# Pair slots of a vision tower's last block: norm weights behind the transposes, rows scattered from the residual, value projection behind the value products

## The chip, the core and the metric

The kernel runs on one core of one Trainium2 chip. A core has TensorE (PE: matmuls and transposes, with PEld its weight loads), VectorE (DVE), ScalarE (ACT), GpSimd (POOL) and SyncE (SP, which here only starts transfers). The engines run their own instruction streams in order and meet at semaphores. The metric is the device time of one execution in microseconds (us), the median of several runs; lower is better.

## The reference, cut to what matters

64 images become 49 tokens of 192 numbers each (a patch embedding), pass a window attention, and then the block that the change touches:

```python
h = tok(x, ...)                                   # patch embedding: (64, 49, 192)
h = h + attn(_layernorm(h), ...)                  # windows attention
h = h + ffn(_layernorm(h), ...)                   # the block below

def ffn(x, ...):                                  # x is the normalised h
    xn = _layernorm(x, norm1_w, norm1_b)
    q, k, v = split(xn @ qkv_w.T + qkv_b)         # 12 heads of 16
    o = softmax(q @ k.T * scale) @ v
    x = x + (o @ proj_w.T + proj_b)
    xn2 = _layernorm(x, norm2_w, norm2_b)         # second norm
    top_vals, top_idx = top_k(xn2 @ w_gate, 2)    # 2 of 8 experts per token
    gates = softmax(top_vals)
    for e in range(8):                            # computed only for the chosen ones in the kernel
        moe += gate[e] * (gelu(xn2 @ W1[e] + b1[e]) @ W2[e] + b2[e])
    return x + moe
```

## The kernel before

The program has four stages. The patch embedding and the window attention come first and are not touched. Then come the **pair slots** (class `Heads`, its methods `gpsimd`, `vector`, `scalar` and `tensor`): 32 pairs of images, a pair being one tile of 128 rows (2 x 64, 49 of each 64 real). After them the **expert tiles**: the token rows, sorted by expert in a DRAM buffer `xs_d`, go through in 56 tiles of 128 rows. Last, every pair fetches its two expert rows per token and adds them to the residual.

The pair slots are a software pipeline written out by hand: `run_slots` calls a function `slot(item)` once per step on every engine, and `item(lag)` is the pair that entered `lag` steps ago. So one slot holds work of up to eight pairs. Slots 0 to 7 and 32 to 38 are unrolled, 8 to 31 are a hardware loop of two slots a turn. Within a slot each engine's order is the order of the lines, and nothing else reorders it:

- lag 0: VectorE takes mean and variance of the residual row block (L619 bn_stats, L633 bn_aggr). GpSimd turns the variance into two inverse roots in six tiny instructions with a drain between each (L507 to L517, "the root chain"), since the block's input is itself a normalised row. VectorE forms the normalised rows (L648), ScalarE scales them again (L804), TensorE transposes them (L943), ScalarE applies the first norm's weight and bias while it copies them out of PSUM, per partition, since the features are on the partitions there (L807).
- lag 1: query and key projections (L898), value projection (L907), ScalarE copies queries (L794) and values (L814) out, VectorE spreads the keys (L644).
- lag 2: scores (L880), maximum and subtraction on VectorE (L624, L629), exponential (L786), transposes (L923, L801), value products (L937), division (L669, L673).
- lag 3: output projection (L887, L783, L903, L904), residual `x2` (L654), second norm's mean and variance (L660, L665), GpSimd's root for it (L536 to L540) and the sum of the two residuals (L542).
- lag 4: ScalarE writes the second norm's rows `xn` without weights (L790). GpSimd multiplies them by the weights (L520) and adds the biases (L532), which lie along the free axis, broadcast over the partitions in the tile `n2`.
- lag 5: transpose of `xn` (L917), copy out (L797), gate logits (L928), and ScalarE copies `xn` twice into `xsrc` (L820).
- lag 6: VectorE picks the two experts and computes the row numbers `dst` (L617 to L684), TensorE counts (L949, L950).
- lag 7: GpSimd appends the token number to `xsrc` (L525) and scatters the rows to `xs_d` in two indirect DMAs (L529).

`xsrc` and `dst` have two buffers, so L820 waits on `scat[u]`, the landing of the scatter that used its buffer before; at lag 5 that is the scatter of the same slot.

In an expert tile SyncE loads 128 rows of `xs_d`, TensorE transposes them (L975, L976), ScalarE copies both halves out of PSUM in one instruction (L834 into `xsT`, one buffer), TensorE multiplies by the first weights (L967, L970), ScalarE applies gelu in six instructions (L844), TensorE multiplies by the second weights (L983), VectorE adds the bias (L759), and GpSimd scatters the rows (L554 to L557). In a slot ScalarE runs the six gelus of one tile and then L834 of the next; L967 of the next slot waits on `e_xT`, which L834 raises:

```python
        def both(item):
            hidden(item)
            expert(item)
```

Of the kernel before, what the change touches and what calls it, by code (L numbers as in the profile page):

```python
# [370 lines left out]
class Heads:  # L371


    def __init__(self, nc, ctx, sb, sem, A, const, ones, colg, x2, kbd, hall, wins, xs_d, yy_d, out, pe1, pt1, pp, s):
# [57 lines left out]
        self.c_x, self.c_xn, self.c_nT, self.d_out, self.d_lg, self.d_oh = sem("c_x"), sem("c_xn"), sem("c_nT"), sem("d_out"), sem("d_lg"), sem("d_oh")  # L432
# [60 lines left out]
    def gpsimd(self, pool):  # L493
# [7 lines left out]
        def slot(item):  # L501
            a, b, c, d = item(0), item(4), item(3), item(7)
# [89 lines left out]
    def vector(self, dve):  # L592
# [6 lines left out]
        dve.drain().then_inc(self.d_src, 1)  # L599
# [7 lines left out]
        def slot(item):  # L607
# [1228 lines left out]
```

## Time and profile before

| | |
|---|---|
| median of 3 runs | 1150.55 us (1149.22 to 1151.24) |
| the profiled execution | 1158.98 us, of which the trace's span is 1157.1 us |
| PE busy | 998.3 us (86% of the span) |
| DVE / ACT / POOL busy | 636.4 / 466.9 / 565.4 us |
| pair slots in the trace | from about 477 to 842 us |
| expert tiles | from about 842 to 1125 us |

Times are microseconds from the span's start. Line numbers (L820) are those of the kernel before, unless the text says otherwise. Busy time of PE is modelled for pipelined matmuls, and a busy engine may still be one that is waited for by nobody; what bounds a stage is the engine whose rows leave no waits.

### The profile page before, as it was taken

What the parts mean: (1) busy time and instruction counts of PE and PEld (TensorE: products, weight loads), DVE (VectorE), ACT (ScalarE), POOL (GpSimd) and SP (SyncE); (2) the same over time, 40 slices, a digit from 0 to 9 for tenths busy, and PEclk for the clock granted to TensorE, in tenths of its full rate; (3) what the DMA queues carried; (4) which work ended last, traced back from release to release, by engine and by line L of the source; (5) the groups of instructions that cost most, each with busy time, mean ns of one, the idle gap of its engine ahead of it and who ended that gap; (6) DMA issues with size and microseconds to landing.
All of it is one profiled execution on the core that took longest, in us unless ns stands there. A gap on an engine that the chain in (4) does not pass through costs nothing.

```text
span 1157.1 us, 24046 instructions
## 1 busy us (share of the span) xinstructions
PE 998.3 (86%) x6992; PEld 854.6 (74%) x6993; DVE 636.4 (55%) x1649; ACT 466.9 (40%) x1172; POOL 565.4 (49%) x1094
## 2 busy tenths in 40 slices
PE   7899999999997987599888888888349999999960
PEld 4789889889975654488677776766339999999950
DVE  7477585575437787466667666665412222222216
ACT  1234323233213444345565555555114444444424
POOL 2578586676421223414666666666504444434330
PEclk9989999999988998799899999998569999999985
DMA  8564662470103300306200000000011111111118
GB/s 356 205 266 189 225 275 95 190 306 34 39 11 62 63 1 0 58 1 266 105 13 16 16 16 16 16 16 19 26 48 38 41 43 43 36 43 42 44 35 253
DMA packets 41701, 103.09 MB, mean 89 GB/s; under 512 B 7046, under 2 KB 28656, under 8 KB 38837
## 3 DMA queue, kind: packets, MB, share of 16 engines
q1 hardware_dynamic: 30085, 88.86, 22.1%
q0 software_dynamic: 5760, 9.68, 2.5%
q10 hardware_dynamic: 5808, 3.96, 1.1%
q8 instruction: 24, 0.39, 0.1%
q14 instruction: 24, 0.20, 0.1%
HBM read 86.30 MB, written 18.32 MB: 90 GB/s over the span
## 4 chain that ended last, share of the span: by engine, by line
PE 35%; POOLq 22%; issue 21%; POOL 7%; DVE 6%; DMA 4%; ACT 2%; DVEq 1%; SPq 1%; ACTq 0%
PE pe L1631 16%; POOLq L561 6%; POOLq L537 4%; PE pe L1640 4%; POOLq L526 2%; DMA x<-yy_d 2%; POOL xn L532 1%; POOLq L539 1%; POOLq L510 1%; POOLq L551 1%; POOL xs_d L529 1%; DVE sc L316 1%; PE pe L183 1%; DMA raw<-in_xw 1%; PE pe L184 1%
## 5 line engine op out<-in xcount | busy, mean ns | idle before, releaser
L1631 PE MATMUL pe<-wm,xm 128*128 128x193 f32 x1008 | 174.1, 331 | 1.7 <-issue 1.7
L1631 PEld LDWEIGHTS pe<-wm,xm 128*128 128x128 f32 x1008 | 168.0, 192 | 6.4 <-issue 6.4
L844 ACT ACTIVATE hT<-pe,eb 128x128 f32<-128x128 f32 x336 | 92.8, 375 | 147.6 <-PE pe L970 147.5
L983 PE MATMUL pp<-w2s,hT 128*128 x672 | 118.5, 326 | 0.0
L983 PEld LDWEIGHTS pp<-w2s,hT 128*128 128x128 f32 x672 | 107.9, 190 | 0.2
L967 PE MATMUL pe<-xsT,ew 128*128 128x128 f32 x672 | 89.4, 284 | 3.3 <-ACT xsT L834 3.3
L967 PEld LDWEIGHTS pe<-xsT,ew 128*128 128x128 f32 x672 | 81.1, 195 | 8.6 <-ACT xsT L834 4.1
L759 DVE TENSOR_TENSOR ys<-pp,b2s 128x192 f32<-128x192 f32 x56 | 20.0, 358 | 121.4 <-PE pp L983 118.5
L529 POOL DMA_INDIRECT xs_d<-xsrc,dst x64 | 65.6, 1025 | 41.7 <-issue 41.7
L557 POOL DMA_INDIRECT yy_d<-ys,yix x56 | 57.2, 1022 | 46.5 <-issue 46.5
L1355 POOL TENSOR_TENSOR sqs<-sqs,sqt 128x448 f32<-128x448 f32 x56 | 67.5, 1205 | 8.0
L563 POOL TENSOR_TENSOR xdum<-xdum 128x1 f32<-128x1 f32 x56 | 21.2, 378 | 101.6 <-issue 85.8
L898 PE MATMUL pp<-xT,wqk 128*96 128x128 f32 x512 | 65.5, 284 | 0.9 <-issue 0.9
L898 PEld LDWEIGHTS pp<-xT,wqk 128*96 128x96 f32 x512 | 62.5, 174 | 1.7 <-issue 1.6
L1251 ACT ACTIVATE sqt<-xm 128x2688 f32<-128x2688 f32 x14 | 34.3, 2447 | 65.5 <-POOL sqs L1355 46.0
L751 DVE COPY eb<-b1s 128x6 f32 x56 | 9.6, 171 | 84.9 <-issue 70.1
L1640 PE MATMUL pe<-ww,wv 128*128 128x193 f32 x300 | 54.9, 333 | 0.0
L644 DVE TENSOR_TENSOR kbd<-pp,const 96x294 f32<-96x294 f32 x128 | 50.2, 451 | 7.6 <-PE pp L898 7.5
L970 PE MATMUL pe<-xsT,ew 64*128 64x128 f32 x672 | 54.0, 294 | 0.0
L880 PE MATMUL pe<-kbd,qT 128*64 128x294 f32 x256 | 47.7, 498 | 7.0 <-issue 3.3
L183 PE MATMUL pe<-wqkv,stg 96*128 96x288 f32 x128 | 44.9, 433 | 9.3 <-ACT stg L228 6.6
L1640 PEld LDWEIGHTS pe<-ww,wv 128*128 128x128 f32 x300 | 51.2, 194 | 0.6 <-issue 0.6
(267 smaller groups left out, 2220.3 us busy)
## 6 DMA issues: line engine op xcount, KB each, us to landing
xm<-in_xm SPq DMA_DIRECT2D x7, 2688.0 KB, 14.0
raw<-in_xwa SPq DMA_DIRECT2D x7, 1792.0 KB, 7.2
raw<-in_xwb SPq DMA_DIRECT2D x7, 1536.0 KB, 11.4
x<-in_x SPq DMA_DIRECT2D x4, 1536.0 KB, 8.6
xs<-xs_d SPq DMA_DIRECT2D x56, 96.5 KB
x<-yy_d SPq DMA_DIRECT2D x8, 672.0 KB
w1s<-in_W SPq DMA_DIRECT2D x1, 4608.0 KB
w2s<-in_W SPq DMA_DIRECT2D x1, 4608.0 KB
```

Source lines behind the costliest of these rows:

```text
L183: mm(y[:, n, 0:288], stg[0:H2, u, 0, s], self.wqkv[0:H2, 0, n * 288:(n + 1) * 288], start=True, stop=False)
L529: g.indirect_dma_start(self.xs_d[:, :], bass.IndirectOffsetOnAxis(ap=self.dst[:, u, k:k + 1], axis=0), self.xsrc[:, u, k], None, bounds_ch ...
L557: g.indirect_dma_start(self.yy_d[:, :], bass.IndirectOffsetOnAxis(ap=self.yix[:, u:u + 1], axis=0), self.ys[:, u], None, bounds_check=2 * ...
L561: pool.drain()
L844: last = f(self.hT[:, u, c], pe1[:, 2 * u + c % 2, (c // 2) * ROWS:(c // 2 + 1) * ROWS], ACT.Gelu, bias=self.b1[:, u, c:c + 1])
L898: last = mm(pp[0:H2, g, m * P:(m + 1) * P], self.wqk[:, h, g * D + m * H2:g * D + (m + 1) * H2], self.xT2[:, h], start=(h == 0), stop=(h = ...
L967: mm(chunk(n), self.w1[:, u, n * P:(n + 1) * P], self.xsT[:, n % 2], start=(n < 2), stop=False, skip_group_check=True)
L970: last = mm(chunk(n), self.w1[r, u, HID + (n // 2) * P:HID + (n // 2 + 1) * P], self.xsT[r, 1 - n % 2], start=False, stop=True, skip_group ...
L983: last = mm(pp[:, u, 0:D], self.hT[:, u, n], self.w2s[:, bass.ds(e, 1), n * D:(n + 1) * D].rearrange("p o d -> p (o d)"), start=(n == 0), ...
L1355: last = nc.gpsimd.tensor_tensor(dst, dst, src[c], ALU.add)
L1631: mm(y[:, 0:D + 1], cell(q, c), wm[:, q, c], start=(q + c == 0), stop=(q == 3 and c == KC - 1))
L1640: mm(y[:, 256:256 + D + 1], wave(wv, wv6, q), ww[:, q], start=(q == 0), stop=(q == 5))
```

## The change

In the pair slots:

- The second norm's weights and biases leave GpSimd: L520 and L532 are gone. `n2` becomes two columns per half of the features, and ScalarE applies them where the features are on the partitions: at the copy behind the transpose for the gate (L797, one instruction of 96x256, becomes two of 96x128), and at the copy behind the expert tile's transposes (L834, one instruction of 128x256, becomes two of 128x128). The rows in `xs_d` are therefore normalised but unweighted.
- ScalarE writes `xsrc` directly from the residual `x2` with the second norm's scale and bias, at lag 6 instead of a copy of `xn` at lag 5. For that GpSimd keeps scale and bias of every pair in a tile `rn`: one more drain and one small copy.
- GpSimd's slot: root chain, scatter, second norm's root, and a drain at its end (the common drain in the middle now belongs to the scatter).
- VectorE's slot: bn_stats and bn_aggr of lag 0 stand first, ahead of the softmax work.
- TensorE's value projection stands behind the value products; ScalarE's query copy then waits for queries and keys only (`a_kk`).
- The loads of `n2` are one transfer instead of two broadcast ones.

```diff
@@ class Heads: gpsimd, in slot
-            a, b, c, d = item(0), item(4), item(3), item(7)
+            a, c, d = item(0), item(3), item(7)
...
-            if b:
-                pool.wait_ge(self.c_x, b[0] + 1)
-                g.tensor_tensor(self.xn[:, b[1]], self.xn[:, b[1]], self.n2[:, 0], ALU.mult)
             if d:
                 i, u, _ = d
-                pool.wait_ge(self.d_src, i + 2)
+                pool.wait_ge(self.d_src, i + 1)
                 pool.wait_ge(self.d_dst, i + 1)
                 g.tensor_copy(self.xsrc[:, u, :, D:DX], ...)
-            pool.drain()
-            if d:
+                pool.drain()
                 for k in range(2):
                     g.indirect_dma_start(self.xs_d[:, :], ...)
-            if b:
-                g.tensor_tensor(self.xn[:, b[1]], self.xn[:, b[1]], self.n2[:, 1], ALU.add).then_inc(self.c_xn, 1)
             if c:
...
-                g.tensor_scalar(st[:, 9:10], st[:, 6:7], st[:, 8:9], -1.0, ALU.mult, ALU.mult).then_inc(self.c_r, 1)
+                g.tensor_scalar(st[:, 9:10], st[:, 6:7], st[:, 8:9], -1.0, ALU.mult, ALU.mult)
+                pool.drain()
+                g.tensor_copy(self.rn[:, bass.ds(i, 1), :].rearrange("p o k -> p (o k)"), st[:, 8:10]).then_inc(self.c_r, 1)
                 rows = [t[:, bass.ds(i, 1), :].rearrange("p o d -> p (o d)") for t in (self.hall, self.x2)]
                 g.tensor_tensor(rows[0], rows[0], rows[1], ALU.add).then_inc(self.res_set, 1)
+            pool.drain()
@@ vector, in slot
             dve.drain()
+            if n0 is not None:
+                v.bn_stats(self.bn[:, 0], row(hall, n0))
             if n6 is not None:
...
                 v.tensor_copy(lg[:], pe1[:, 3, 256:256 + E]).then_inc(self.d_lgo, 1)
+            dve.drain()
             if n0 is not None:
-                v.bn_stats(self.bn[:, 0], row(hall, n0))
-            dve.drain()
+                v.bn_aggr(st[:, 0:2], self.bn[:, 0]).then_inc(self.a_var, 1)
...
-            if n0 is not None:
-                v.bn_aggr(st[:, 0:2], self.bn[:, 0]).then_inc(self.a_var, 1)
@@ scalar, in slot
             if n4 is not None:
-                act.wait_ge(self.d_src, n4)
                 act.wait_ge(self.c_r, n4 + 1)
...
             if n1 is not None:
-                act.wait_ge(self.a_qkv, n1 + 1)
+                act.wait_ge(self.a_kk, n1 + 1)
                 f(self.qT[0:H2], pp[0:H2, 0, 0:2 * P].rearrange("p (h n) -> p h n", h=2), ACT.Copy).then_inc(self.a_q, 1)
             if n5 is not None:
                 act.wait_ge(self.c_nT, n5 + 1)
-                f(self.xnT2[0:H2], pe1[0:H2, 3, 0:2 * P].rearrange("p (h n) -> p h n", h=2), ACT.Copy).then_inc(self.d_out, 1)
+                for h in range(2):
+                    last = f(self.xnT2[0:H2, h], pe1[0:H2, 3, h * P:(h + 1) * P], ACT.Identity, bias=colg[:, h, 6:7], scale=colg[:, h, 5:6])
+                last.then_inc(self.d_out, 1)
...
             if n1 is not None:
+                act.wait_ge(self.a_qkv, n1 + 1)
                 act.wait_ge(self.b_pv, n1)
...
-            if n5 is not None:
-                u = item(5)[1]
-                act.wait_ge(self.c_xn, n5 + 1)
-                act.wait_ge(self.scat[u], 32 * item(5)[2])
-                f(self.xsrc[:, u, :, 0:D], self.xn[:, u:u + 1].to_broadcast([P, 2, D]), ACT.Copy).then_inc(self.d_src, 1)
             if n6 is not None:
...
+                act.wait_ge(self.scat[u], 32 * item(6)[2])
+                f(self.xsrc[:, u, :, 0:D], self.x2[:, bass.ds(n6, 1), :].to_broadcast([P, 2, D]), ACT.Identity, bias=col(n6, 1), scale=col(n6, 0)).then_inc(self.d_src, 1)
@@ scalar, expert tile
             act.wait_ge(self.e_T, i + 3)
-            f(self.xsT[:], pt1[:, u, 0:2 * ROWS].rearrange("p (h n) -> p h n", h=2), ACT.Copy).then_inc(self.e_xT, 1)
+            for h in range(2):
+                last = f(self.xsT[:, h], pt1[:, u, h * ROWS:(h + 1) * ROWS], ACT.Identity, bias=self.n2[:, h, 1:2], scale=self.n2[:, h, 0:1])
+            last.then_inc(self.e_xT, 1)
@@ tensor, in slot
-            if n1 is not None:
-                for h in range(2):
-                    last = mm(pp[:, 0, 256:256 + D], self.xT2[:, h], self.wqk[:, h, 2 * D:3 * D], start=(h == 0), stop=(h == 1))
-                last.then_inc(self.a_qkv, 1)
...
-                pe.wait_ge(self.c_xn, n5 + 1)
+                pe.wait_ge(self.c_x, n5 + 1)
...
                 last.then_inc(self.b_pv, 1)
+            if n1 is not None:
+                pe.wait_ge(self.a_q, n1 + 1)
+                for h in range(2):
+                    last = mm(pp[:, 0, 256:256 + D], self.xT2[:, h], self.wqk[:, h, 2 * D:3 * D], start=(h == 0), stop=(h == 1))
+                last.then_inc(self.a_qkv, 1)
```

ScalarE's order in the expert tiles, one tile inside the hardware loop (hT is the gelu's output, xsT the transposed token rows). Before:

```order
L844 ACTIVATE hT<-pe,eb 128x128 x6
L833 REGISTER_ALU
L834 ACTIVATE xsT<-pt 128x256
L107 REGISTER_ALU
L107 COMPARE_AND_BRANCH
```

and changed (n is the tile `n2` with weights and biases):

```order
L848 ACTIVATE hT<-pe,eb 128x128 x6
L835 REGISTER_ALU
L837 ACTIVATE xsT<-pt,n 128x128 x2
L107 REGISTER_ALU
L107 COMPARE_AND_BRANCH
```

The copy behind the six gelus is now two instructions of half the width with operands for scale and bias.

GpSimd's slot inside the loop (st holds one column per intermediate). Before:

```order
L517 TENSOR_TENSOR st<-st,const 128x1
L520 TENSOR_TENSOR xn<-xn,n 128x192
L523 REGISTER_ALU
L525 ISA
L525 COPY xsrc<-const 128x2
L529 DMA xs_d<-xsrc,dst 26240x193 x2
L532 TENSOR_TENSOR xn<-xn,n 128x192
L535 REGISTER_ALU
L536 TENSOR_TENSOR st<-st,const 128x1
L538 TENSOR_TENSOR st<-st,const 128x1
L540 TENSOR_SCALAR st<-st 128x1
L542 ISA
```

and changed:

```order
L518 TENSOR_TENSOR st<-st,const 128x1
L521 REGISTER_ALU
L523 ISA
L523 COPY xsrc<-const 128x2
L526 DMA xs_d<-xsrc,dst 26240x193 x2
L530 REGISTER_ALU
L531 TENSOR_TENSOR st<-st,const 128x1
L533 TENSOR_TENSOR st<-st,const 128x1
L535 TENSOR_SCALAR st<-st 128x1
L537 ISA
L537 COPY rn<-st 128x2
L539 ISA
```

The two 192-wide instructions are gone, the copy into `rn` is new, and everything else keeps its place.

VectorE's slot inside the loop, from its start (bn and st hold the statistics, lg the gate logits, mx and pm the softmax). Before:

```order
L617 COPY lg<-pe 128x8
L619 ISA
L619 BN_STATS bn<-hall 128x6
L624 TENSOR_REDUCE mx<-pe 128x12
L626 MAX m<-lg 128x8
L629 TENSOR_TENSOR pm<-pe,mx 128x12x49
L633 BN_AGGR st<-bn 128x2
```

and changed:

```order
L610 BN_STATS bn<-hall 128x6
L614 REGISTER_ALU
L615 REGISTER_ALU
L616 COPY lg<-pe 128x8
L619 BN_AGGR st<-bn 128x2
L623 TENSOR_REDUCE mx<-pe 128x12
L625 MAX m<-lg 128x8
```

The variance that GpSimd's root chain waits for no longer stands behind the two softmax passes, the first of which waits for the scores.

## Rows read from the trace of the kernel before

**Rows 1.** Stretches: us, busy PE, PEld, DVE, ACT, POOL (instructions), granted clock, DMA.

```profile
590.00:795.00 205.00, 178.75 (x1608) 146.20 (x1607) 141.54 (x530) 122.11 (x341) 142.66 (x319) 0.96 0.05 16
870.00:1110.00 240.00, 240.00 (x1987) 222.93 (x1986) 65.05 (x156) 101.90 (x370) 96.95 (x261) 1.00 0.14 41
```

**Rows 2.** Timeline, POOL, one slot: start, us, what, idle before and its releaser.

```profile
611.67 0.19 POOL L507 TENSOR_TENSOR st<-st,const 128x1 f32<-128x1 f32 x1
612.00 0.55 POOL L509 TENSOR_TENSOR st<-st,const 128x1 f32<-128x1 f32 x1
...
614.22 0.59 POOL L520 TENSOR_TENSOR xn<-xn,n 128x192 f32<-128x192 f32 x1
614.75 0.22 POOL L525 COPY xsrc<-const 128x2 f32 x1
615.83 1.08 POOL L529 DMA_INDIRECT xs_d<-xsrc,dst  x1 [0.87 <-issue]
617.22 0.97 POOL L529 DMA_INDIRECT xs_d<-xsrc,dst  x1 [0.30 <-issue]
618.21 0.60 POOL L532 TENSOR_TENSOR xn<-xn,n 128x192 f32<-128x192 f32 x1
...
619.94 0.57 POOL L538 TENSOR_TENSOR st<-st,const 128x1 f32<-128x1 f32 x1 [0.98 <-issue]
620.68 0.26 POOL L540 TENSOR_SCALAR st<-st 128x1 f32<-128x1 f32 x1 [0.17 <-issue]
620.90 0.59 POOL L542 TENSOR_TENSOR hall<-hall,x  x1
621.44 0.19 POOL L507 TENSOR_TENSOR st<-st,const 128x1 f32<-128x1 f32 x1
```

**Rows 3.** Timeline, all engines, a slot of the tail.

```profile
829.13 0.98 POOL L529 DMA_INDIRECT xs_d<-xsrc,dst  x1 [0.30 <-issue]
...
830.86 0.19 POOL L525 COPY xsrc<-const 128x2 f32<-128x2 f32 x1 [0.76 <-DVE dst L684]
...
831.54 0.52 ACT L820 ACTIVATE xsrc<-xn 128x384 f32<-128x384 f32 x1 [3.57 <-DMA xs_d<-xsrc,dst]
...
832.38 0.98 POOL L529 DMA_INDIRECT xs_d<-xsrc,dst  x1 [1.33 <-issue]
```

**Rows 4.** Timeline, POOL, the root chain's starts in slots 9 and 10.

```profile
571.58 0.19 POOL L507 TENSOR_TENSOR st<-st,const 128x1 f32<-128x1 f32 x1 [1.31 <-DVE st L633]
...
582.71 0.19 POOL L507 TENSOR_TENSOR st<-st,const 128x1 f32<-128x1 f32 x1 [1.50 <-DVE st L633]
```

**Rows 5.** Timeline, DVE and POOL, the tail: row numbers, one scatter's copy.

```profile
810.99 0.23 DVE L684 TENSOR_SCALAR dst<-df,const 128x2 int32<-128x2 f32 x1
...
821.00 0.19 POOL L525 COPY xsrc<-const 128x2 f32<-128x2 f32 x1
...
834.04 0.23 DVE L684 TENSOR_SCALAR dst<-df,const 128x2 int32<-128x2 f32 x1
```

**Rows 6.** Timeline, all engines, an expert tile at full clock.

```profile
1002.59 1.66 ACT L844 ACTIVATE hT<-pe,eb 128x128 f32<-128x128 f32 x6 [2.66 <-PE pe L970]
...
1004.10 0.42 ACT L834 ACTIVATE xsT<-pt 128x256 f32<-128x256 f32 x1
...
1004.57 1.42 PEld L967 LDWEIGHTS pe<-xsT,ew 128*128 128x128 f32 x12
```

**Rows 7.** Timeline, all engines, the first expert tile.

```profile
852.56 0.38 ACT L834 ACTIVATE xsT<-pt 128x256 f32<-128x256 f32 x1 [19.88 <-PE pt L976]
853.00 2.93 PE L967 MATMUL pe<-xsT,ew 128*128 128x128 f32 x12 [0.47 <-ACT xsT L834]
```

**Rows 8.** Timeline, ACT, two copies with scale and bias operands.

```profile
606.41 0.80 ACT L807 ACTIVATE xT<-pt,colg 96x128 f32<-96x128 f32 x2 [0.52 <-PE pt L943]
```

**Rows 9.** Timeline, DVE and POOL, the end of the expert tiles.

```profile
1105.94 0.36 DVE L759 TENSOR_TENSOR ys<-pp,b2s 128x192 f32<-128x192 f32 x1 [2.20 <-PE pp L983]
...
1108.64 0.19 POOL L554 TENSOR_TENSOR xdum<-xdum 128x1 f32<-128x1 f32 x1 [0.22 <-issue]
```

More of the change, by code:

```diff
@@ L415, in __init__ @@
         self.wgate = sb("wgate", [P, 2, E])
-        self.n2 = sb("n2", [P, 2, D])
+        self.n2 = sb("n2", [P, 2, 2])
         self.gates = sb("gates", [P, NP, 2])
         self.egs = sb("egs", [P, NP])
+        self.rn = sb("rn", [P, NP, 2])
         self.meta = sb("meta", [1, 3, NT], I32)
@@ L431, in __init__ @@
         self.c_T, self.c_out, self.c_proj, self.c_var, self.c_r = sem("c_T"), sem("c_out"), sem("c_proj"), sem("c_var"), sem("c_r")
-        self.c_x, self.c_xn, self.c_nT, self.d_out, self.d_lg, self.d_oh = sem("c_x"), sem("c_xn"), sem("c_nT"), sem("d_out"), sem("d_lg"), sem("d_oh")
+        self.c_x, self.c_nT, self.d_out, self.d_lg, self.d_oh = sem("c_x"), sem("c_nT"), sem("d_out"), sem("d_lg"), sem("d_oh")
         self.d_rank, self.d_eg, self.d_dst, self.d_src = sem("d_rank"), sem("d_eg"), sem("d_dst"), sem("d_src")
@@ L598, in vector @@
         dve.drain().then_inc(self.xs_used, 2)
-        dve.drain().then_inc(self.d_src, 1)
         dve.wait_ge(self.s["base_ld"], 64)
@@ L776, in scalar, with row, col @@
         act.wait_ge(self.init, 2)
+        def row(t, i):
+            return t[:, bass.ds(i, 1), :].rearrange("p o d -> p (o d)")
+        def col(i, k):
+            return self.rn[:, bass.ds(i, 1), k:k + 1].rearrange("p o k -> p (o k)")
         def slot(item):
@@ L787, in slot @@
             if n4 is not None:
-                act.wait_ge(self.d_src, n4)
                 act.wait_ge(self.c_r, n4 + 1)
-                f(self.xn[:, item(4)[1]], self.x2[:, bass.ds(n4, 1), :].rearrange("p o d -> p (o d)"), ACT.Identity,
-                  bias=self.st[:, 9:10], scale=self.st[:, 8:9]).then_inc(self.c_x, 1)
+                f(self.xn[:, item(4)[1]], row(self.x2, n4), ACT.Identity, bias=col(n4, 1), scale=col(n4, 0)).then_inc(self.c_x, 1)
             if n1 is not None:
-                act.wait_ge(self.a_qkv, n1 + 1)
+                act.wait_ge(self.a_kk, n1 + 1)
                 f(self.qT[0:H2], pp[0:H2, 0, 0:2 * P].rearrange("p (h n) -> p h n", h=2), ACT.Copy).then_inc(self.a_q, 1)
@@ L815, in slot @@
                 last.then_inc(self.a_v, 1)
-            if n5 is not None:
-                u = item(5)[1]
-                act.wait_ge(self.c_xn, n5 + 1)
-                act.wait_ge(self.scat[u], 32 * item(5)[2])
-                f(self.xsrc[:, u, :, 0:D], self.xn[:, u:u + 1].to_broadcast([P, 2, D]), ACT.Copy).then_inc(self.d_src, 1)
             if n6 is not None:
+                u = item(6)[1]
                 act.wait_ge(self.d_oh, n6 + 1)
-                m8 = self.m8[:, item(6)[1]]
+                m8 = self.m8[:, u]
                 f(self.egs[:, bass.ds(n6, 1)], m8[:, 0:1], ACT.Exp, bias=m8[:, 1:2], scale=-1.0).then_inc(self.d_eg, 1)
+                act.wait_ge(self.scat[u], 32 * item(6)[2])
+                f(self.xsrc[:, u, :, 0:D], self.x2[:, bass.ds(n6, 1), :].to_broadcast([P, 2, D]), ACT.Identity, bias=col(n6, 1), scale=col(n6, 0)).then_inc(self.d_src, 1)
         run_slots(act, NP, 8, slot)
@@ L890, in slot @@
                 if isinstance(n1, int) and n1 == 0:
-                    pe.wait_ge(self.hw_ld, 16 * 7)
+                    pe.wait_ge(self.hw_ld, 16 * 6)
                 pe.wait_ge(self.a_xT, n1 + 1)
@@ L991, in load_weights @@
         for dst, src in ((self.wqk[0:H2], A["qkvT"]), (self.wqk[H2:H2 + 1, 1], A["qkvb"]), (self.wproj[0:H2], A["projT"]),
[L992 to L993 removed]
+                         (self.wproj[H2:H2 + 1, 1], A["projb"]), (self.wgate[0:H2], A["wgate"]), (self.n2[:], A["n2"])):
             sp.dma_start(dst, src).then_inc(self.hw_ld, 16)
@@ L1065, in build @@
         wqkv = sb("wqkv", [H2 + 1, 2, 3 * D])
-        colg = sb("colg", [H2, 2, 5])
+        colg = sb("colg", [H2, 2, 7])
         e2 = ExitStack()
@@ L1766, in lay_out @@
     g["inb"] = f["L0_attn_inb"][None]
-    cols = [f[n][:, None] for n in ("L0_attn_ln_g", "L0_attn_ln_b", "L0_attn_mob", "L0_ffn_norm1_w", "L0_ffn_norm1_b")]
+    cols = [f[n][:, None] for n in ("L0_attn_ln_g", "L0_attn_ln_b", "L0_attn_mob", "L0_ffn_norm1_w", "L0_ffn_norm1_b", "L0_ffn_norm2_w", "L0_ffn_norm2_b")]
     g["cols"] = halves(np.concatenate(cols, 1))
@@ L1777, in lay_out @@
     g["projb"] = f["L0_ffn_proj_b"][None]
-    g["n2"] = np.stack([f["L0_ffn_norm2_w"], f["L0_ffn_norm2_b"]])
+    n2 = np.stack([f["L0_ffn_norm2_w"], f["L0_ffn_norm2_b"]], 1)
+    g["n2"] = np.ascontiguousarray(np.stack([n2[:P], n2[LOW:]], 1))
     g["wgate"] = halves(f["L0_ffn_w_gate"])
```

2 lines of the change are left out of this document (removed).

## Prediction

> **What bounds the kernel now.** I read the stretches first. In the pair slots (590 to 795 us) no engine is full: PE is busy 178.75 of 205 us (87%), POOL 142.66, DVE 141.54, ACT 122.11. In the expert tiles (870 to 1110 us) PE is busy 240.00 of 240.00 us [rows 1]. So the first stage needs another view, and the second seems plain.
>
> For the pair slots I read POOL's timeline through one slot [rows 2]. It starts at 611.67 and the next at 621.44: 9.77 us. The idle stretches in it stand only behind drains and before indirect DMAs, all marked "issue"; nothing in it waits for another engine's semaphore. POOL's own instructions, drains included, are the slot. The other engines wait for its root chain.
>
> One stretch needs a closer look: after the second scatter DMA ends (617.22 + 0.97 = 618.19) L538 starts only at 619.94, idle for 0.98, while an ordinary drain between two tiny instructions costs 0.14 (611.67 + 0.19 to 612.00) [rows 2]. The tail shows what the drain waits for [rows 3]. A scatter's DMA ends at 829.13 + 0.98 = 830.11. ACT's L820, which waits for its landing, starts at 831.54. POOL's copy L525 ends at 831.05 and the next DMA starts at 832.38, 1.33 later; in the ordinary slot that gap is 0.86 (614.97 to 615.83). The 0.47 more puts the end of that drain at about 831.5, where the scatter landed. I conclude that a drain behind an indirect DMA ends with the landing, some 1.4 to 1.6 us after the DMA's end, whatever small work stands between.
>
> For the expert tiles I read one tile on ACT and PE [rows 6]. Six gelus run from 1002.59 to 1004.25, L834 runs 1004.10 to 1004.52, and the weight load of L967 starts at 1004.57, 0.05 behind it. Where PE undoubtedly waited for this copy, in the first tile, the distance is 0.06 (852.94 to 853.00) [rows 7]. So although PE shows no idle time here, L967 starts as early as L834 permits and no earlier. The loop L967, L970, gelus, L834, L967 has no slack; it happens to be as long as PE's own work. One turn of it takes 4.59: L844 had been idle for 2.66 before 1002.59, so the L834 before ended at 999.93, and this one ends at 1004.52 [rows 6].
>
> **The change part by part**, against the profiled execution (1158.98 us, span 1157.1); the median of the runs is 1150.55, and I carry the difference over to it.
>
> *POOL's slot in the loop* [rows 2]. Removed: L520, which takes 614.75 - 614.22 = 0.53 of the chain, and L532. The latter lies between the scatter's end and its landing, and the drain behind it waits for the landing, so it is worth 0 (at most 0.54 a slot, were the drain a fixed cost). Added: behind L540 (0.26) a drain (0.14) and the copy to `rn`, for which I take L525's 0.22, so +0.40; and at the slot's end L542 no longer overlaps with L507, 0.59 + 0.14 in place of 0.54, +0.19. The new slot: 2.55 (root) + 1.08 + 1.39 (to the second DMA) + 2.72 (to L538) + 0.74 + 0.40 + 0.22 + 0.73 = 9.83 against 9.77. I take +0.07. 205 us hold 21 such slots: **+1.4**; ends -11 (L532 worth its 0.54) and +4 (each new drain 0.1 dearer).
>
> *Early variance.* In slots 9 and 10 POOL waited 1.31 and 1.50 us for L633, since PE was late with the scores and bn_aggr stood behind both softmax passes [rows 4]. It now stands ahead of them, and both waits go. Slot 7, the first with a scatter, begins earlier too, but its drain waits for the landing behind the loads of the expert weights, so I give it only 0.2. **-3.0**; ends 0 and -5. In the other loop slots variance was early already. What is late next is POOL itself.
>
> *ACT's and PE's moves in the slots.* L820 no longer waits for the same slot's scatter; onT, queries and PE's projection come earlier, but wait for nothing that POOL doesn't set. The four value matmuls are only moved: PE has 13% idle [rows 1], 1.25 us a slot. The second activation for the gate's transposes adds 0.38 (below) before the logits and the value products, inside the same 1.25 us. **0**; if that cover were gone, 0.38 x 24 slots = 9.
>
> *The tail*, slots 32 to 38. Before, every slot passed through scatter, landing, L820, transpose copy, logits, VectorE's table, scatter. Now `xsrc` waits only for the scatter of the slot before. I start at 811.2, where VectorE has the row numbers of pair 27 (810.99 + 0.23) [rows 5]. A POOL slot without the root chain is 9.83 - 2.55 = 7.28, so the copy of pair 28 comes at 818.6, not 821.00 [rows 5]. First DMA at +1.08, second done at +1.39 + 0.97, landed +1.43: 823.5. The next starts 0.72 later (0.86 less 0.14), and lands at 824.2 + 1.39 + 0.97 + 1.43 = 828.0. Then the buffer of `dst` for pair 31 is free and L684 ends the table at 828.1 instead of 834.04 [rows 5]; the expert tiles' table hangs on it. **-5.9**; ends 0 and -9.
>
> *ACT's copy in the expert tiles.* One copy of 0.42 [rows 6] becomes two with operands for scale and bias. The nearest row is L807, the same kind at 96x128: two take 0.80 [rows 8]. So xsT is ready 0.38 later. PE has no slack there, and the delay returns every tile, through L970 and the gelus. 56 tiles, less two at the start in which other waits hide it: 54 x 0.38 = **+20.5**. Lower end: spaced like the gelus, 1.66 / 6 = 0.28 each [rows 6], +0.13 a tile, 7; upper end two full 0.53 of a wide one, 33. I take L807, as it differs only in 96 for 128 partitions.
>
> The Trainium skill speaks against this part too. "ScalarE: Activation LUTs", section "What ACT_TABLE_LOAD costs", gives an instruction with immediate scale and bias 186 ns plus 0.833 ns a column, about 93 ns more for each per-partition operand, and an overlap of about 93 ns between neighbours. By it the copy would be 0.40 and the pair 0.86, a difference of 0.47 a tile and an estimate of 25 us; L807 measured 0.80 for the pair, and the sum goes by that.
>
> *End of the expert tiles.* POOL's scatter runs behind: L759 ends at 1106.30 and its L554 starts at 1108.64, without a wait for another engine [rows 9]. With tiles 0.38 longer POOL catches up, and its 2.3 us of lag don't stand at the end. **-2.0**; ends 0 and -2.3.
>
> Sum: +1.4 - 3.0 + 0 - 5.9 + 20.5 - 2.0 = +11.0. Profiled about 1170, median 1150.55 + 11 = **1161.5 us**.
>
> **The rivals.**
>
> 1. *The wider slot pays.* The drain behind the scatter is a fixed cost, and L532 frees its 0.54 in every one of the 24 slots with a scatter and a root chain: -13 more, 1148.5 us. For it: L538's gap is nearly the same in all slots. Against: rows 3, where the gap grew exactly to the landing.
> 2. *The copy is hidden: not slower.* PE would have started L967 at 1004.57 from its own queue, and there is room behind it (L983 still drains then), so that a later xsT only eats it. Place: L967's wait. Price: the +20.5 and the -2.0 both go, 1143 us. It decides if PE can take 0.38 us later weights without a later L970. For it: PE 240.00 busy of 240.00. Against: the 0.05, equal to the distance in a proven wait.
> 3. *The pair is cheap.* Behind gelus the two activations are spaced like gelus: +0.13 a tile, 7 in place of 20.5, 1148 us.
> 4. *The clock falls in the expert tiles.* PE now pauses 0.38 in every 4.97 us. In the pair slots, at 87% busy, the granted clock is 0.96 (8% of the time at the level of 1.2 GHz), in the expert tiles 1.00 (2.4 GHz all through) [rows 1]. If the pauses bring the experts to 0.96, 22 us are spent at the lower level, at about 9.2 us a tile (twice 4.59) in place of 4.97: +10, 1171.5 us. The Trainium skill, "TensorE: Matmul & The Clock Gate", section "A second HAM failure mode: psum-queue depth-cycling", tells of short pauses between groups of matmuls that make the clock oscillate; the trace's pair slots agree, but with pauses three times as long.
>
> **How the numbers follow.** Forecast 0.66 (own range 1155 to 1167), rival 1 0.10, rival 2 0.08, rival 3 0.08, rival 4 0.08. Range 1147 to 1170. A difference under 0.2% (2.3 us) can't be told from none. Faster than 1148.2: rival 2 and half of rivals 1 and 3, 0.17. Within: the other halves, 0.09. Slower: 0.74.
>
> **What would show it.** Each step has its row: L837 as two instructions in about 0.80 and a new wait of PE for it, in 50 tiles or more, 0.3 to 0.4 each; tiles 4.97 apart instead of 4.59; POOL's slot still 9.7 to 9.9 with the first drain behind the scatter now longer (about 1.5 from DMA end to L533); no wait of the root chain in slots 9 and 10; the table's end 8 to 9 us earlier (front and tail together, less the loop's 1.4). The forecast is wrong if tiles stay 4.6 apart or POOL's slot is at 9.3.

## The result, and the profile after

| | before | changed |
|---|---|---|
| median | 1150.89 us (4 runs, 1149.22 to 1154.87) | 1182.28 us (4 runs, 1180.32 to 1183.58) |
| ratio | | 1.0266, 95% interval 1.0235 to 1.0297 |
| profiled execution | 1158.98, span 1157.1 | 1183.58, span 1181.7 |

The changed kernel is slower by 31.4 us; forecast were 11, so direction and largest term were right and the size was not. The stages below are cut at GpSimd's root chains (of pairs 0, 11, 31), the first write of `xsT`, the last of `ys` and the end. The profiled execution of before was 8.1 us above its median, so a second execution with the same code stands beside it (the kernel of the second experiment, which alters the expert tiles alone; in brackets, for the expert tiles and the end, stand the times of the experiment without L532, whose expert tiles are those of before):

| stage | before | before, again | changed | changed less before again | forecast |
|---|---|---|---|---|---|
| to pair 0's root chain | 484.08 | 485.32 | 486.76 | +1.4 | 0 |
| slots 0 to 10 | 108.29 | 105.59 | 108.19 | +2.6 | -3.0 |
| 20 loop slots | 192.90 | 192.49 | 200.96 | +8.5 | +1.4 |
| tail | 67.29 | 64.33 | 61.36 | -3.0 | -5.9 |
| expert tiles | 265.51 | (264.77) | 288.03 | +23.3 | +20.5 |
| end | 39.03 | (37.41) | 36.40 | -1.0 | -2.0 |

These differences add up to 31.8, close to the medians' 31.4; against the first profile they give 24.6. Each stage is read from single executions, and pair 0's root chain starts anywhere from 482.4 to 486.9 us in the executions of this document, though no experiment touches what stands ahead of it. The two executions of before differ by 3.0 us in slots 7 to 10 (42.39 and 39.36) and by 3.0 in the tail, and two of my terms rested on just these stretches of the first.

Stretches of the changed kernel, which answer [rows 1] (columns as there):

```profile
595.00:795.00 200.00, 173.61 (x1499) 136.06 (x1498) 130.84 (x494) 126.38 (x338) 116.51 (x279) 0.93 0.04 15
880.00:1120.00 240.00, 229.48 (x1818) 203.74 (x1814) 60.33 (x143) 113.22 (x384) 89.55 (x243) 1.00 0.13 39
```

PE now pauses in the expert tiles, 10.5 us in 240, at a granted clock of 1.00. GpSimd's slot, timeline, against [rows 2]:

```profile
603.98 0.59 POOL L539 TENSOR_TENSOR hall<-hall,x  x1
605.22 0.19 POOL L508 TENSOR_TENSOR st<-st,const 128x1 f32<-128x1 f32 x1 [0.65 <-issue]
...
610.24 0.98 POOL L526 DMA_INDIRECT xs_d<-xsrc,dst  x1 [0.30 <-issue]
611.22 0.23 POOL L531 TENSOR_TENSOR st<-st,const 128x1 f32<-128x1 f32 x1
612.77 0.57 POOL L533 TENSOR_TENSOR st<-st,const 128x1 f32<-128x1 f32 x1 [1.32 <-issue]
613.51 0.27 POOL L535 TENSOR_SCALAR st<-st 128x1 f32<-128x1 f32 x1 [0.17 <-issue]
614.01 0.19 POOL L537 COPY rn<-st 128x2 f32 x1 [0.23 <-issue]
614.16 0.59 POOL L539 TENSOR_TENSOR hall<-hall,x  x1
614.99 0.19 POOL L508 TENSOR_TENSOR st<-st,const 128x1 f32<-128x1 f32 x1 [0.23 <-issue]
```

L533 starts 1.55 after the DMA's end, with no L532 between: the drain ends with the landing, as predicted. But the next slot starts 0.83 us after L539 in one slot and 1.24 in the other, where before it was 0.54 [rows 2]. Both idle stretches are marked "issue". The rows of GpSimd's queue show what fills them. In the changed kernel the loop's branch and the register instruction of the root chain's wait start behind L539:

```profile
L107 POOLq COMPARE_BRANCH  x1: 53/53/53, 604.7 to 604.7; - x1
L507 POOLq ALU_OP  x1: 32/32/32, 605.1 to 605.1; - x1
```

In the kernel before they started while L542 still ran (620.90 to 621.49) [rows 2]:

```profile
L107 POOLq COMPARE_BRANCH  x1: 53/53/53, 620.9 to 620.9; - x1
L506 POOLq ALU_OP  x1: 32/32/32, 621.3 to 621.3; - x1
```

The slots alternate between 9.77 and 10.26 us. An expert tile, which answers [rows 6]:

```profile
1002.29 0.84 ACT L837 ACTIVATE xsT<-pt,n 128x128 f32<-128x128 f32 x2
...
1003.18 1.41 PEld L972 LDWEIGHTS pe<-xsT,ew 128*128 128x128 f32 x12 [0.51 <-ACT xsT L837]
...
1005.78 1.66 ACT L848 ACTIVATE hT<-pe,eb 128x128 f32<-128x128 f32 x6 [2.66 <-PE pe L975]
...
1007.30 0.49 ACT L837 ACTIVATE xsT<-pt,n 128x128 f32<-128x128 f32 x1
```

L837 to L837 is 5.01. The pair takes 0.84 where one copy took 0.42, and ACT is again idle 2.66 between copy and gelus, as in [rows 6]: the loop grew by just the copy's growth. The waits show PE behind it in nearly every tile (55 waits, 32.3 us in all, the longest 3.7):

```profile
PEld pe L972 <- ACT xsT L837: 32.3, 55, 3.7
```

GpSimd's timeline at the end of the expert tiles, against [rows 9], shows that it has caught up and waits 2.70 for VectorE:

```profile
1143.76 0.18 POOL L552 TENSOR_TENSOR xdum<-xdum 128x1 f32<-128x1 f32 x1 [2.70 <-DVE ys L756]
```

### The profile page after: what moved, and what is told of

Read it like the earlier page. It is cut to its first block, busy times and chain, and to the rows that moved or that the text cites. A ratio compares the mean times of both kernels' runs of the same rounds, so it can differ in the third digit from the quotient of the medians.

```text
span 1181.7 us, 24216 instructions
## 1 busy us (share of the span) xinstructions
PE 1017.5 (86%) x6992; PEld 854.4 (72%) x6993; DVE 634.6 (54%) x1649; ACT 509.7 (43%) x1260; POOL 537.8 (46%) x1062
## 4 chain that ended last, share of the span: by engine, by line
PE 47%; POOLq 13%; issue 13%; ACT 11%; DVE 6%; DMA 4%; POOL 3%; DVEq 1%; SPq 1%; ACTq 0%
PE pe L1635 16%; PE pe L972 7%; ACT hT L848 6%; PE pe L1644 4%; PE pe L975 4%; POOLq L532 4%; ACT xsT L837 3%; DMA x<-yy_d 2%; POOLq L534 1%; POOLq L540 1%; POOLq L511 1%; DVE sc L316 1%; PE pe L183 1%; DMA raw<-in_xw 1%; POOL xs_d L526 1%
## 5 line engine op out<-in xcount | busy, mean ns | idle before, releaser
L972 PE MATMUL pe<-xsT,ew 128*128 128x128 f32 x672 | 92.4, 289 | 16.0 <-ACT xsT L837 16.0
L972 PEld LDWEIGHTS pe<-xsT,ew 128*128 128x128 f32 x672 | 81.7, 196 | 32.3 <-ACT xsT L837 32.3
L555 POOL DMA_INDIRECT yy_d<-ys,yix x56 | 68.1, 1215 | 46.4 <-issue 46.4
L561 POOL TENSOR_TENSOR xdum<-xdum 128x1 f32<-128x1 f32 x56 | 10.3, 185 | 100.9 <-issue 87.2
L837 ACT ACTIVATE xsT<-pt,n 128x128 f32<-128x128 f32 x112 | 47.1, 495 | 19.2 <-PE pt L981 19.2
## 6 DMA issues: line engine op xcount, KB each, us to landing
raw<-in_xwb SPq DMA_DIRECT2D x7, 1536.0 KB, 10.8
```

What stands on the lines that cost most here:

```text
L555: g.indirect_dma_start(self.yy_d[:, :], bass.IndirectOffsetOnAxis(ap=self.yix[:, u:u + 1], axis=0), self.ys[:, u], None, bounds_check=2 * ...
L837: last = f(self.xsT[:, h], pt1[:, u, h * ROWS:(h + 1) * ROWS], ACT.Identity, bias=self.n2[:, h, 1:2], scale=self.n2[:, h, 0:1])
L972: mm(chunk(n), self.w1[:, u, n * P:(n + 1) * P], self.xsT[:, n % 2], start=(n < 2), stop=False, skip_group_check=True)
```

## The experiments

"Before" and "changed" are the two kernels. Ratios are to before, run beside the experiment. The changed kernel gave 1.0266 at first and 1.0288 when it ran again with experiments 10 to 12; the two intervals overlap. A stage's time comes from one execution of each kernel.

**1. One copy again (changed kernel).**

```diff
-            for h in range(2):
-                last = f(self.xsT[:, h], pt1[:, u, h * ROWS:(h + 1) * ROWS], ACT.Identity, bias=self.n2[:, h, 1:2], scale=self.n2[:, h, 0:1])
-            last.then_inc(self.e_xT, 1)
+            f(self.xsT[:], pt1[:, u, 0:2 * ROWS].rearrange("p (h n) -> p h n", h=2), ACT.Copy).then_inc(self.e_xT, 1)
```

> The changed kernel, with the expert tile's xsT written by one ACT copy of 128x256 again instead of two activations of 128x128 with scale and bias (leaves out: the second norm's weights and biases in the expert tiles). Theory A (the copy stands on the expert loop's chain without slack; the trace of the changed kernel has tiles 0.43 us longer, 55 of them, less the 2 us by which GpSimd catches up): 1182.3 - 23 + 2 = about 1161 us, tiles 4.58 apart again. Rival B (the tiles are longer for another reason, such as PE's own order or the clock): over 1175 us and tiles still about 5.0 apart.

The time is 1158.53 us, 1.0063 (1.0043 to 1.0082), which is 23.8 us less. The expert tiles take 264.25 us, as before.

**2. The pair alone (before).** The opposite edit.

> The kernel before, with xsT in the expert tiles written by two activations of 128x128 with per-partition scale and bias (columns of the broadcast weights serve as operands, so the values scaled are those of features 0 and 1 everywhere). Theory A: the pair alone costs what it costs in the changed kernel, 55 x 0.42 = 23, less 2 at the end: 1150.9 + 21 = about 1172 us, tiles about 5.0 apart. Rival B (it costs more in the changed kernel, through what the pair slots leave behind): under 1165 us.

The time is 1175.59 us, 1.0207 (1.0189 to 1.0224), which is 24.7 us more; the expert tiles take 287.73. The pair costs 24 us in either kernel, as theory A has it.

**3. `xsT` on VectorE (changed kernel).** ACT's `expert` goes; in VectorE's, behind the weight copies:

```diff
+                dve.wait_ge(self.e_T, i + 3)
+                for h in range(2):
+                    last = v.tensor_scalar(self.xsT[:, h], self.pt1[:, u, h * ROWS:(h + 1) * ROWS], self.n2[:, h, 0:1], self.n2[:, h, 1:2], ALU.mult, ALU.add)
+                last.then_inc(self.e_xT, 1)
```

> The changed kernel, with xsT's two halves written by VectorE (scale and bias as tensor_scalar, in VectorE's order behind the weight copies of the tile) instead of by ACT. Nothing is left out. Theory A (L972 waits for ACT because the pair stands behind six gelus; VectorE is 26% busy here): the wait goes, tiles are at most as long as before, 4.58 or less: about 1158 us or under. Rival B (VectorE's pair comes late itself, behind its own waits, or PE's own work is 5 us a tile): 1170 us or more.

The time is 1150.74 us, 0.9996 (0.9982 to 1.0010): 31.5 us less, more than the pair had cost. The timeline shows why:

```profile
1001.26 1.65 ACT L843 ACTIVATE hT<-pe,eb 128x128 f32<-128x128 f32 x6 [2.87 <-PE pe L969]
1001.33 2.12 PE L982 MATMUL pp<-w2s,hT 128*128 x12
...
1001.67 0.73 DVE L753 TENSOR_SCALAR xsT<-pt,n 128x128 f32<-128x128 f32 x2 [0.20 <-PE pt L975]
1003.12 1.47 PEld L966 LDWEIGHTS pe<-xsT,ew 128*128 128x128 f32 x12
```

`xsT` is ready at 1002.40, beside the gelus, and PE follows from its own queue, without a wait between 870 and 1110 us. Tiles, by VectorE's writes of `ys`, are 4.52 and 4.53 apart; before they were 4.49 and 4.68 by turns, 4.59 on average. The expert tiles take 257.31 us.

**4. The copy into `rn` on ACT (changed kernel).**

```diff
-                pool.drain()
-                g.tensor_copy(self.rn[:, ...], st[:, 8:10]).then_inc(self.c_r, 1)
+                # ACT, ahead of the write of xn; GpSimd waits for c_x of the pair before
+                f(row(self.rn, n4), self.st[:, 8:10], ACT.Copy)
```

> The changed kernel, with the copy of scale and bias into rn moved from GpSimd (with the drain ahead of it) to ACT, just ahead of the write of xn; GpSimd waits for ACT's read of the pair before. Nothing is left out. Theory A (GpSimd's chain is the slot; drain, register work and copy are 0.5 to 0.6 us of it in 24 slots): 1182.3 - 13 = about 1169 us. Rival B (the slot is set by another engine now, or the copy was hidden): within 3 us of 1182.

The time is 1167.36 us, 1.0129 (1.0110 to 1.0148): 14.9 us less. The 20 loop slots take 189.54 instead of 200.96: 0.57 a slot.

**5. No drain at the end of the slot (changed kernel).** The last `pool.drain()` of GpSimd's slot is deleted.

> The changed kernel without GpSimd's drain at the end of the pair slot, so that L539 runs beside the next slot's first instruction as L542 did before. Theory A (the drain exposes the slot's register work and, in every second slot, the loop's branch: 0.84 and 1.26 us from L539's start to L508, where before it was 0.55): 0.3 and 0.7 us alternately, 24 slots, about -12: 1170 us, the pair of slots near 19.1 us. Rival B (my prediction's value for it, 0.19 a slot, and the register work shows up elsewhere): -4, 1178 us, the two slots of a turn still unequal.

The time is 1173.52 us, 1.0144 (1.0101 to 1.0186), against 1.0266 and 1.0288 with the drain. The 20 loop slots take 189.90 instead of 200.96, which is 0.55 a slot, and they no longer alternate (9.44 to 9.64). The whole gained less than the slots, since the expert tiles took 295.10 in this execution instead of 288.03, for a reason told in the last section. Timeline:

```profile
607.76 0.59 POOL L539 TENSOR_TENSOR hall<-hall,x  x1
608.31 0.19 POOL L508 TENSOR_TENSOR st<-st,const 128x1 f32<-128x1 f32 x1
```

From L539 to L508 it is 0.55 again, so the alternation came from the drain: behind it the queue's instructions (L507's in every slot, and L107's branch in every second one) no longer run under L539.

**6. That drain added to before.**

> The kernel before with one drain more, at the end of GpSimd's pair slot behind L542. Theory A (the drain exposes register work and the loop's branch): 0.3 and 0.7 us alternately, +12 over 24 slots: about 1163 us, slots alternating by about 0.4 us. Rival B (0.19 a slot): +4.5, 1155.5 us, slots equal.

The time is 1166.83 us, 1.0082 (1.0050 to 1.0113), which is 9.5 us more. The loop slots take 206.03, 0.7 a slot more than before. They alternate between 9.9 and 10.28, as theory A has it:

```profile
633.54 0.60 POOL L542 TENSOR_TENSOR hall<-hall,x  x1
634.37 0.19 POOL L507 TENSOR_TENSOR st<-st,const 128x1 f32<-128x1 f32 x1 [0.23 <-issue]
...
643.41 0.59 POOL L542 TENSOR_TENSOR hall<-hall,x  x1
644.65 0.19 POOL L507 TENSOR_TENSOR st<-st,const 128x1 f32<-128x1 f32 x1 [0.65 <-issue]
```

Five of the 20 are 10.8 to 11.1 long. Their granted clock is 0.82 to 0.84, and the root chain behind each waits 1.1 to 1.5 us for VectorE's late variance; no slot at a clock of 1.00 waits for it.

**7. No L532 (before).**

> The kernel before without L532, GpSimd's add of the second norm's bias behind the scatter (leaves out that bias; the semaphore that followed it is raised by L520). Theory A (L532 lies between the scatter's DMA and its landing, which the next drain waits for): 0 to -1 us, and the idle time before L538 grows from 0.8-1.0 to 1.3-1.5. Rival B (the drain is a fixed cost and L532 pays its 0.54): -13 us, 1138 us.

The time is 1157.58 us, 1.0006 (0.9984 to 1.0028), and the loop slots are unchanged (192.70). The removed 0.6 turns into idle time of the drain, 1.32 instead of 0.79 to 0.98 [rows 2]; from the DMA's end to the instruction behind the drain it is 1.55 to 1.6 in most slots with and without L532. The prediction's first rival is out.

```profile
605.20 0.97 POOL L529 DMA_INDIRECT xs_d<-xsrc,dst  x1 [0.30 <-issue]
606.19 0.21 POOL L534 TENSOR_TENSOR st<-st,const 128x1 f32<-128x1 f32 x1
607.72 0.57 POOL L536 TENSOR_TENSOR st<-st,const 128x1 f32<-128x1 f32 x1 [1.32 <-issue]
```

**8. Early variance alone (before).**

```diff
             dve.drain()
+            if n0 is not None:
+                v.bn_stats(self.bn[:, 0], row(hall, n0))
...
             dve.drain()
+            if n0 is not None:
+                v.bn_aggr(st[:, 0:2], self.bn[:, 0]).then_inc(self.a_var, 1)
```

> The kernel before with only VectorE's variance moved to the start of the slot (bn_stats and bn_aggr of lag 0 first). Theory A (the waits of 1.31 and 1.50 us in slots 9 and 10 of the first profile came with a low-clock spell that fell there; another profile of the same pair slots has 0 and 0.16; and what slots 4 to 7 gain the first scatter's drain gives back): within 1 us of 1150.9, with slot 7's drain longer by what slots 0 to 7 are shorter (2.6 us). Rival B (the prediction's value): -3 us, 1148 us.

The time is 1154.57 us, 1.0003 (0.9974 to 1.0033), no change within 0.3% (12 runs, 1152.42 to 1167.53). Slots 0 to 6 take 62.33 instead of 65.90, or of 66.23 in the other execution of before; slots 7 to 10 take 44.80 instead of 42.39, or of 39.36. Slot 7's timeline:

```profile
552.79 0.97 POOL L529 DMA_INDIRECT xs_d<-xsrc,dst  x1 [0.30 <-issue]
...
558.78 0.57 POOL L538 TENSOR_TENSOR st<-st,const 128x1 f32<-128x1 f32 x1 [4.25 <-issue]
```

The DMA engines are full until about 557 (shares of 0.98 to 1.11 in stretches of 2 us, then 0.15), by the load of the expert weights, and the drain ends only behind that, so it takes what the slots had gained. Slot 8's is long too (2.81), and so it is in the changed kernel (2.58); why, I did not find.

**9. The changed kernel again, beside the next three.**

> The changed kernel itself once more, on the chip of its neighbours here, to have the difference between whole kernels and experiments on one chip. Theory: ratio to before 1.024 to 1.030 as first measured; tiles 4.92 and 5.11 us alternately without any of the 5.4 us that the run without the end-of-slot drain showed in 13 tiles. If such longer tiles appear here too, they belong to the chip and not to that edit.

The time is 1186.87 us, 1.0288 (1.0257 to 1.0320). It does have tiles of 5.4 us, as the run without the end drain had, so those don't belong to that edit; the last section has more.

**10. Edits 3, 4 and 5 together (changed kernel).**

> The changed kernel with three edits together: xsT written by VectorE, the copy of scale and bias into rn on ACT, no drain at the end of GpSimd's slot. Nothing is left out. Theory A (the three add up: -31.5, -14.9 and -14 as measured apart): 1182.3 - 60.4 = about 1122 us, ratio to before 0.975, pair slots 8.93 us apart. Rival B (below 9.4 us a slot PE, busy 8.7 us of it, or VectorE's variance takes over as the bound, and the loop gives half): about 1130 us, ratio 0.982, GpSimd's root chain waits for VectorE again.

The time is 1126.78 us, 0.9767 (0.9744 to 0.9790): faster than both kernels. The loop slots take 9.08 us on average, without a wait for VectorE. Twenty of them take 181.56 instead of 200.96, 0.97 a slot: the drain and the copy are worth less together than the 0.55 and 0.57 that they are worth apart.

**11. `xsT` on VectorE (before).**

> The kernel before with only its expert copy xsT moved to VectorE, as two tensor_scalar by 1.0. Nothing is left out. Theory A (ACT's copy behind the gelus made the expert loop 4.585 long where PE alone needs 4.525; VectorE hides it): 265 - 257.5 = 7.5 us less, about 1143 us, ratio 0.9935. Rival B (PE was the bound before, 240 of 240 us busy, and the 4.525 of the other run belongs to the rest of the change): within 2 us of before.

The time is 1147.32 us, 0.9932 (0.9906 to 0.9958), and the expert tiles take 259.04, as theory A has it. So ACT's copy did bound the expert tiles of before.

**12. Value projection back (changed kernel).**

> The changed kernel with TensorE's value projection back at its old place, ahead of the transposes for the gate, and ACT's query copy waiting for it as before. Nothing is left out. Theory A (the move is worth 0, since GpSimd sets the slot): within 2 us of the changed kernel, ratio 1.025 to 1.028. Rival B (the move gives PE or ACT time that is used in the first slots or the tail): 1185 us or more, ratio over 1.030.

The time is 1189.34 us, 1.0291 (1.0262 to 1.0320), beside 1.0288: the move is worth 0 within 0.3%. In this execution the granted clock from 595 to 795 us is 0.85, against 0.93 in the first of the changed kernel, and the 20 loop slots take 201.60 against 200.96: where GpSimd's chain is the slot, the lower clock cost next to nothing.

**13. Late variance (changed kernel).** Experiment 8 reversed.

> The changed kernel with VectorE's variance back behind the softmax passes, as before. Nothing else is changed. Theory A (what slots 0 to 7 gain by the early variance the drain behind the first scatter gives back, since that scatter lands only when the expert weights are in): slots 0 to 7 take 66 instead of 63.3 us, slots 7 to 11 some 40 to 42 instead of 44.7, in sum 0 to -2: ratio to before 1.024 to 1.029. Rival B (the prediction: the early variance is worth 3 us): +3, ratio 1.030 or more.

The time is 1189.40 us, 1.0293 (1.0254 to 1.0331), beside 1.0288 with the early variance: worth 0 within 0.3% here too. The stages moved less than expected (64.55 and 43.24 us).

**14. No L520 (before).**

> The kernel before without L520, GpSimd's multiplication by the second norm's weights (leaves those weights out). Theory A (L520 stands on GpSimd's chain with 0.53 us in each of 24 slots with a scatter): slot 9.11 instead of 9.64, -12.5 us, ratio 0.989. Rival B (another engine, VectorE's late variance above all, is the bound once the slot falls below 9.6): -4 or less, ratio 0.996 or more, and GpSimd's L507 waits for VectorE's L633 in the loop.

The time is 1164.41 us, 1.0072 (1.0050 to 1.0093). Rival B's ratio (0.996 or more) and its wait of L507 for VectorE are there, but neither theory had it slower than before. The slots are 9.05 in some stretches and 10.6 in others. First come two slots as stretches, with the granted clock as the third value from the end, then rows of their timeline:

```profile
604.49:615.83 11.34, 10.23 (x90) 9.38 (x90) 7.11 (x29) 5.86 (x17) 6.20 (x15) 0.89 0.04 13
615.83:625.01 9.18, 8.42 (x80) 6.96 (x79) 7.16 (x28) 6.29 (x17) 6.18 (x14) 1.00 0.05 17
```

```profile
603.61 3.57 PE L897 MATMUL pp<-xT,wqk 128*96 128x128 f32 x16
...
615.83 0.19 POOL L507 TENSOR_TENSOR st<-st,const 128x1 f32<-128x1 f32 x1 [1.61 <-DVE st L632]
...
625.01 0.19 POOL L507 TENSOR_TENSOR st<-st,const 128x1 f32<-128x1 f32 x1
```

At the level of 1.2 GHz L897 takes 3.57 us (1.91 in the next slot), the scores come late, VectorE's variance stands behind them, and GpSimd waits 1.61 for it. The loop as a whole (592 to 770 us) ran at a clock of 0.89, against 0.96 in [rows 1], and over the whole program the ten runs had 0.903 to 0.915, the thirteen of before beside them 0.923 to 0.930. Whether the low clock makes the waits or the waits keep the clock low, this run alone doesn't separate.

**15. Rows at lag 5 again (changed kernel).** `xsrc` is copied from `xn` behind the same slot's scatter.

> The changed kernel with the rows of xsrc copied from xn at lag 5 again, behind the landing of the same slot's scatter, with the wait that guards xn. Nothing is left out. Theory A (rows at lag 6 shorten the tail by 4 us and nothing else): the tail, from the last root chain to the first expert copy, 65 instead of 61.2 us, slots unchanged: +4, ratio 1.030 to 1.032. Rival B (the tail's gain has another source, or the loop is touched too): tail within 1 us of 61.2, or ratio over 1.035.

The time is 1187.37 us, 1.0274 (1.0236 to 1.0312), and the tail takes 61.58 us. Theory A falls: the rows' new lag is worth 0.2 us of the tail, though ACT waits for the landing in each slot.

**16. All three edits, late variance.**

> The version with all three edits (xsT on VectorE, rn on ACT, no end-of-slot drain), with the variance back behind the softmax passes. Nothing is left out. Theory A (with slots of 9.08 us the late variance comes 1 to 2 us after GpSimd is ready for it, in every slot): +20 to +35, ratio 0.995 to 1.008, GpSimd's root chain waits for VectorE in each slot. Rival B (the early variance is worth nothing here too): within 3 us, ratio 0.974 to 0.980.

The time is 1132.19 us, 0.9795 (0.9756 to 0.9833): the ratio lies in rival B's range, and its interval overlaps that of experiment 10. Most loop slots are 9.0 to 9.3, two are 9.91 and 10.76, with waits of 0.81 and 1.70 for the variance. So with the other engines in the changed order the late variance costs little even in slots of 9.1; what in that order makes the difference to experiment 14 was not separated, and this version with the value projection back as well was not run.

**17. All three edits, value projection back.**

> The version with all three edits (xsT on VectorE, rn on ACT, no end-of-slot drain), with TensorE's value projection back at its old place and ACT's query copy waiting for it. Nothing is left out. Theory A (the projection's move is what makes the loop through TensorE, ACT and VectorE short enough for slots of 9.1 us): ratio to before 0.985 or more, slots over 9.3 us on average, GpSimd waiting for VectorE in some of them. Rival B (the early variance alone does it): within 3 us of the 1126.8 of that version, ratio 0.974 to 0.980.

The time is 1126.46 us, 0.9780 (0.9743 to 0.9817): no difference, as rival B has it.

**18. No L520, early variance (before).** Edits 8 and 14.

> The kernel before without L520 (leaves out the second norm's weights) and with VectorE's variance first in its slot. Theory A (the late variance alone kept the 0.53 us of L520 from paying): slots near 9.1 us at either clock, no wait of GpSimd for the variance, -10 us, ratio 0.989 to 0.993. Rival B (at the lower clock the loop through TensorE and ACT is the bound wherever the variance stands): slots of 10 us and more remain at the lower clock, ratio 1.000 or more.

The time is 1133.28 us, 0.9840 (0.9815 to 0.9865). The loop slots are 9.00 to 9.16 but for one of 9.54, at either clock, and the tail is 61.16. A stretch about as long as a slot, at the lower clock:

```profile
647.40:656.50 9.10, 8.52 (x72) 6.62 (x71) 6.42 (x25) 5.49 (x16) 6.16 (x14) 0.81 0.05 17
```

The loop ran at a clock of 0.96 again, so a shorter slot of GpSimd doesn't lower the clock by itself. The 20 loop slots take 181.50 against 193.12 in experiment 8, 0.58 a slot for L520. In the kernel before, L520's removal costs 0.7% without the early variance and gains 1.6% with it.

## Why the prediction missed the size

- *ACT's copy in the expert tiles, +20.5: mechanism right, size off.* The loop without slack was real (experiments 1, 2, 11). The pair took 0.84, or 0.42 more than the copy, where I had taken 0.38 from L807's 96 partitions [rows 8]; 55 x 0.42 = 23. The 0.47 that the Trainium skill's "ScalarE: Activation LUTs", section "What ACT_TABLE_LOAD costs", gave was 0.05 too high, and L807 was 0.04 too low.
- *GpSimd's slot in the loop, +1.4: this step failed.* Measured were +8.1 to +8.5. I priced the end drain by instruction lengths, at 0.19; it cost 0.55 (experiment 5), as the drain exposes the register instruction and the branch that the queue worked off under L542 before. The copy into `rn` cost 0.57, not 0.40 (experiment 4). Together they cost 0.97 (experiment 10) in place of 0.59; less L520's 0.53 that is 0.44 a slot, or 8.8 us in 20. L532 at 0 was right (experiment 7), and so was L520's 0.53 (0.58 in experiment 18), but in before's order of the other engines it pays only where the variance is early (experiments 14 and 18).
- *Early variance, -3.0: failed.* The waits of 1.31 and 1.50 [rows 4] stood in a spell at a granted clock of 0.69 and 0.85 that this one execution had in those slots; the other execution of before has none and 0.16. A spell like it can fall elsewhere: experiment 11, whose slots are those of before, has three loop slots of 10.8 to 11.3 at 0.80 to 0.84, with waits of 1.66, 1.12 and 1.44 for VectorE. The 0.2 that I credited for slot 7 was right in kind, since its drain took most of what the slots ahead gained, or more (experiment 8). Its use in before's order is another: it lets a shorter slot of GpSimd pay at the lower clock.
- *The moves of the value projection, 0:* This was right within 0.4% (experiments 12 and 17).
- *The tail, -5.9: the number is that of the first profile, the cause is wrong.* Against two other executions of before's slots (64.33 and 66.36 us) it is 3.0 and 5.0, and not the lag of the rows (experiment 15). Before without L520 and with the early variance has 61.16 (experiment 18), and 63.79 without L520 alone (experiment 14); but the changed kernel keeps its tail with the late variance (61.11, experiment 13) and loses it with the value projection back (64.12, experiment 12), which experiment 17, at 58.44, doesn't bear out. The cause stays open. The table of row numbers, which I expected to end 8 to 9 us earlier, ended at 838.87 instead of 834.04, 4.8 later; my own terms added up to 7.5 earlier, not 8 to 9.
- *End, -2.0: not shown.* It is 2.6 shorter against the first profile and 1.0 against the experiment without L532. GpSimd did catch up, but so it did in experiment 2, whose end of 37.52 is no shorter than that 37.41.
- *Rival 1 (the drain a fixed cost), rival 2 (hidden copy), rival 3 (cheap pair), rival 4 (clock down in the experts):* All are false. L532's removal is worth nothing, PE waits in 55 tiles, the pair takes 0.84, and the clock stays at 1.00.

With 23.3 for the pair, 8.5 for the loop and 2.6 for the first slots, -3.0 and -1.0 behind them, the same sum gives +30.4, and the 1.4 ahead of the slots makes it 31.8. That is the table told again, and no test of it.

## What to carry to other kernels

A drain at the end of a slot is not priced by its own length: read the idle time that stands behind drains near register work and branches, in slots with the loop's branch and in slots without it. Before a wait is counted as a gain, look at the granted clock of its slot and at a second execution. An edit on a loop without slack costs its full length per turn; an engine that is idle at that moment can take the work, which here gave back 31.5 us for a pair that had cost 24.

## What was not expected of the hardware

In the changed kernel run again (experiment 9), 9 of 55 tiles were 5.41 to 5.45 us long by the writes of `ys`, in its first execution none. ACT's gelus start 0.5 later there, behind the same PE group:

```profile
928.61 1.66 ACT L848 ACTIVATE hT<-pe,eb 128x128 f32<-128x128 f32 x6 [2.65 <-PE pe L975]
930.12 0.84 ACT L837 ACTIVATE xsT<-pt,n 128x128 f32<-128x128 f32 x2
...
932.56 0.94 PE L975 MATMUL pe<-xsT,ew 64*128 64x128 f32 x12
...
934.12 1.66 ACT L848 ACTIVATE hT<-pe,eb 128x128 f32<-128x128 f32 x6 [3.16 <-PE pe L975]
```

It cost 5 us of expert tiles (293.00 against 288.03). Experiments 5, 12, 13 and 15 had it too, with expert tiles of 292.58 to 295.10; experiments 2 and 4 did not, though they are recorded for the same chip as 9 and 12, so the chip alone doesn't decide it. It was absent wherever one copy or VectorE wrote `xsT`. Its cause stays open, and so does slot 8's long drain in experiment 8. The best version's loop ran at a granted clock of 1.00 throughout, with PE busy 152.56 of 178 us:

```profile
592.00:770.00 178.00, 152.56 (x1486) 129.55 (x1483) 123.26 (x488) 121.44 (x351) 110.03 (x255) 1.00 0.05 17
```
